# A transformer layer in fp32 on one core: transposes moved between projections, stores queued later, one probability slot given for two activation slots

## What is computed

```
xn  = (x - mean) / sqrt(var + 1e-5)                        per token
q, k, v = split(xn @ w_qkv + b_qkv);  16 heads of 16
a   = softmax(q k^T / 4, keys j >= i only) @ v
s   = a @ w_out + b_out
h   = 2 relu(s0 * [xn, -xn] @ (+-1 from k0))               512 -> 1024
h   = 2 relu(s1 * h @ (+-1 from k1))                       1024 -> 1024
g   = silu(s2 * h @ (+-1 from k2))                         1024 -> 256
out = x + s * g
```

## Time and profile before

| | |
|---|---|
| median of three runs | 2287.67 us (2287.02 to 2289.31) |
| the profiled execution | 2290.6 us, of which its span 2288.8 us |
| PE busy | 2219.8 us, 97% of the span |
| DVE, ACT, POOL busy | 78%, 69%, 40% |
| chain that ended last, by engine | PE 85%, DMA 4%, DVE 4%, issue 2%, POOL 2%, ACT 1%, SP queue 1% |
| first chain item of the projections | DMA a_xs<-L_attn_x, 3% of the span |
| moved | 193.31 MB, mean 84 GB/s |

### The profile page before, as it was taken

The page is one execution under the profiler, slowest core; times in us unless marked ns, Lnnn a source line. Parts: engine busy times, 40 slices in busy tenths (PEclk is TensorE's granted clock), DMA queues, the critical chain, the costliest instruction groups (busy, mean ns, idle before and its releaser), DMA issues.

```text
span 2288.8 us, 60916 instructions
## 1 busy us (share of the span) xinstructions
PE 2219.8 (97%) x23760; PEld 1579.6 (69%) x23760; DVE 1783.3 (78%) x4484; ACT 1569.0 (69%) x3199; POOL 908.2 (40%) x1080
## 2 busy tenths in 40 slices
PE   7998999999999999999999999999999999999987
PEld 6787776667676766666666666777666767776653
DVE  7774788888888878788878878787878788887742
ACT  5663467777777776667777767777777677777554
POOL 1004434333442454335344443444354443445534
PEclk9999999999999999999999999999999999999988
DMA  8995111111121312222222213122222222123132
GB/s 299 350 330 178 32 33 43 43 53 44 42 54 30 99 38 78 56 55 68 58 81 62 77 46 98 39 81 51 67 72 57 67 62 82 48 83 89 53 94 83
DMA packets 157844, 193.31 MB, mean 84 GB/s; under 512 B 65276, under 2 KB 102076, under 8 KB 157560
## 3 DMA queue, kind: packets, MB, share of 16 engines
q1 hardware_dynamic: 156600, 189.41, 27.1%
q10 hardware_dynamic: 960, 0.00, 0.0%
HBM read 112.13 MB, written 76.14 MB: 82 GB/s over the span
## 4 chain that ended last, share of the span: by engine, by line
PE 85%; DMA 4%; DVE 4%; issue 2%; POOL 2%; ACT 1%; SPq 1%; ACTq 0%; POOLq 0%; DVEq 0%
PE b_ps L1423 26%; PE b_pv_ps L1389 22%; PE b_ps L1360 15%; PE b_ps L1370 12%; PE b_ps L1419 5%; DMA a_xs<-L_attn_x 3%; PE b_ps L1444 2%; PE a_qk_ps L291 1%; DVE b_part_max L1535 1%; DVE a_stats L397 1%; DVE a_qk_parts L435 1%; PE b_ps L1377 1%; ACT b_u L1509 1%; ACT b_probs L1478 1%; POOL b_u_lo L1292 0%
## 5 line engine op out<-in xcount | busy, mean ns | idle before, releaser
L1478 ACT ACTIVATE b_probs<-b_ps 128x512 f32<-128x512 f32 (+3 forms) x2560 | 1248.9, 540 | 566.4 <-PE b_ps L1360 532.5
L1535 DVE TENSOR_REDUCE b_part_max<-b_ps 128x1 f32<-128x512 f32 x1536 | 967.8, 682 | 187.4 <-PE b_ps L1370 181.8
L1360 PE MATMUL b_ps<-k_qst,k_kst 50*128 50x512 f32 (+3 forms) x2560 | 907.6, 389 | 8.7 <-DMA k_qst<-b_max_parts 7.2
L1370 PE MATMUL b_ps<-k_kst,k_qst 48*128 48x512 f32 (+3 forms) x2560 | 900.6, 391 | 8.7 <-DMA k_qst<-qk_parts 2.9
L1360 PEld LDWEIGHTS b_ps<-k_qst,k_kst 50*128 50x128 f32 x2560 | 445.4, 186 | 254.5 <-issue 93.0
L1532 DVE CUSTOM_DVE_ANT_0 b_ps<-b_ps,k_mask 128x512 f32<-128x512 f32 (+3 forms) x1024 | 481.5, 515 | 159.3 <-PE b_ps L1370 149.4
L1423 PE MATMUL b_ps<-b_u_hi,k_w 64*128 64x256 f32 x4096 | 594.1, 282 | 1.1 <-ACT b_u L1509 0.7
L1423 PE MATMUL b_ps<-b_u_lo,k_w 64*128 64x256 f32 x4096 | 587.3, 280 | 0.0
L1389 PE MATMUL b_pv_ps<-b_probs,k_vst 128*32 128x512 f32 (+3 forms) x5120 | 567.6, 539 | 3.6 <-issue 2.7
L1370 PEld LDWEIGHTS b_ps<-k_kst,k_qst 48*128 48x128 f32 x2560 | 438.6, 185 | 105.4 <-issue 28.1
L1423 PEld LDWEIGHTS b_ps<-b_u_hi,k_w 64*128 64x128 f32 x4096 | 464.5, 187 | 23.1 <-issue 6.4
(11 more groups left out here) (102 smaller groups left out, 1906.5 us busy)
## 6 DMA issues: line engine op xcount, KB each, us to landing
qk_parts<-a_qk_parts SPq DMA_DIRECT2D x64, 512.0 KB, 3.8
k_kst<-qk_parts SPq DMA_DIRECT2D x384, 64.0 KB, 2.3
k_qst<-qk_parts SPq DMA_DIRECT2D x384, 64.0 KB, 2.3
a_xs<-L_attn_x SPq DMA_DIRECT2D x16, 512.0 KB, 6.1
xn_T<-a_xT SPq DMA_DIRECT2D x16, 512.0 KB, 5.9
v_plain<-a_v_out SPq DMA_DIRECT2D x16, 512.0 KB, 5.7
k_xf<-xn_T SPq DMA_DIRECT2D x32, 256.0 KB, 3.3
b_v_in<-v_plain SPq DMA_DIRECT2D x64, 128.0 KB, 2.7
```

The source lines that it names most:

```text
L1360: pe.matmul(dst[:, 0:cols], keys, qst[rows, c, pair, 0:cols], start=True, stop=True).then_inc(s_ready, 1)
L1370: pe.matmul(dst[:, 0:CHUNK - k1], qst[rows, c, pair, i * P:(i + 1) * P], kst[rows, k_slot(kc, g % 2), pair, k1:CHUNK], start=True, stop=Tr ...
L1478: act.activation(probs[:, s % P_SLOTS, h, 0:cols], ps[:, banks[place, 0][0], 0:cols], ACT.Exp, scale=HD ** -0.5).then_inc(exp_done, 1)
L1535: dve.tensor_reduce(dst, src, AX_X, ALU.max).then_inc(ring_read, 1)
```

## The change

In the first stage the transposes of chunk i+1 and the high copies that go with them move in between the q/k groups (before m = 2; in chunk 0 before m = 3), and DVE's `split_x(i + 1)` moves from behind `deviation` to in front of `low(2)`. A token tile is turned when it is normalised, not when all four are. The first x is loaded in four transfers with a semaphore each; the split of chunk 0 and the whole copy of it come before the statistics and the deviation of chunk 1. In the second stage SP's stores of the gate and of the result leave the place of the work that makes them: they come 3 and 4 steps later, or just before the next "fetch", "fetch_last" or "gate" if that is sooner. `P_SLOTS` goes from 5 to 4, `U_SLOTS` from 2 to 4.

```diff
--- before.py
+++ after.py
@@ -170,6 +170,7 @@
         w_ready = sem("w_ready")
         blank = sem("blank")
         x_loaded = [sem(f"x_loaded{n}") for n in range(2)]
+        x_first = [sem(f"x_first{t}") for t in range(TT)]
         waited = sem("waited")
         ln_stat, ln_aggr, ln_step = sem("ln_stat"), sem("ln_aggr"), sem("ln_step")
         var_ready, std_ready = sem("var_ready"), sem("std_ready")
@@ -187,6 +188,10 @@
 
         x_t = x.rearrange("b s h -> (b s) h")
 
+        def turn_at(i):
+
+            return KH if i > 0 else 2 * KH - 1
+
         def over_chunks(chunk):
 
             for i in range(NCHUNK):
@@ -198,7 +203,8 @@
                 src = x_t[j * CHUNK:(j + 1) * CHUNK, :].rearrange("(t p) h -> p t h", p=P)
                 sp.dma_start(xs[par][:], src).then_inc(x_loaded[par], DMA)
 
-            load_x(0, 0)
+            for t in range(TT):
+                sp.dma_start(xs[0][:, t, :], x_t[t * P:(t + 1) * P, :]).then_inc(x_first[t], DMA)
             sp.dma_start(wqkv[:], w_qkv.rearrange("(k p) f -> p k f", p=P)).then_inc(wqkv_loaded, DMA)
             load_x(1, 1)
             sp.dma_start(k0s[:], k0.rearrange("(a k p) f -> p (a k) f", a=2, p=P)
@@ -269,15 +275,16 @@
         @block.tensor
         def _(pe):
             def turn(j, par):
-                pe.wait_ge(xn_ready, (j + 1) * TT)
                 if j > 0:
 
                     pe.wait_ge(xT_copied, j * KH)
-                for ft in range(KH):
-                    for t in range(TT):
+                for t in range(TT):
+                    pe.wait_ge(xn_ready, j * TT + t + 1)
+                    for ft in range(KH):
                         mm = pe.transpose(turned[:, ft, t * P:(t + 1) * P], xs[par][:, t, ft * P:(ft + 1) * P],
                                           kept.identity[:])
-                    mm.then_inc(turned_ready, 1)
+                        if t == TT - 1:
+                            mm.then_inc(turned_ready, 1)
 
             products = [(k, w, part) for k in range(KH)
                         for w, part in ((wqkv_hi, xT_hi), (wqkv_hi, xT_lo), (wqkv_lo, xT_hi))]
@@ -285,14 +292,14 @@
             def chunk(i, half, par, left):
                 pe.wait_ge(xT_low, (i + 1) * KH)
                 for m in range(2 * KH):
+                    if m == turn_at(i) and left:
+                        turn(i + 1, 1 - par)
 
                     pe.wait_ge(qk_low, i * 2 * KH + m + 1)
                     for n, (k, w, part) in enumerate(products):
                         mm = pe.matmul(qk_ps[:, m], w[:, k, m * P:(m + 1) * P], part[par][:, k, :],
                                        start=(n == 0), stop=(n == len(products) - 1))
                     mm.then_inc(qk_ready, 1)
-                if left:
-                    turn(i + 1, 1 - par)
                 for u in range(VU):
                     pe.wait_ge(v_done, i * VU + u + 1)
                     for t in range(2):
@@ -321,6 +328,8 @@
                 act.sem_inc(qk_stored[par], QK_STORES * DMA)
                 act.sem_inc(v_stored[par], DMA)
                 act.sem_inc(xT_stored[par], DMA)
+
+            act.sem_inc(x_loaded[0], DMA)
 
             def std_of(j):
                 act.wait_ge(var_ready, j + 1)
@@ -356,13 +365,13 @@
             def chunk(i, half, par, left):
                 act.wait_ge(qk_stored[par], (half + 1) * QK_STORES * DMA)
                 for m in range(2 * KH):
+                    if m == turn_at(i) and left:
+                        copy_high(i + 1, 1 - par)
                     act.wait_ge(qk_ready, i * 2 * KH + m + 1)
                     act.activation(qk_parts[par][:, m, HI, :], qk_ps[:, m], ACT.Identity,
                                    bias=bqk[:, m:m + 1]).then_inc(qk_high, 1)
                 if left > 1:
                     std_of(i + 2)
-                if left:
-                    copy_high(i + 1, 1 - par)
                 act.wait_ge(v_stored[par], (half + 1) * DMA)
                 for u in range(VU):
                     act.wait_ge(v_ready, i * VU + u + 1)
@@ -377,8 +386,8 @@
             act.wait_ge(wqkv_loaded, DMA)
             act.activation(wqkv_hi[:], wqkv[:], ACT.Copy).then_inc(wqkv_split, 1)
             copy_high(0, 0)
+            copy_whole(0, 0, 0)
             std_of(1)
-            copy_whole(0, 0, 0)
             act.wait_ge(consts, 3)
             act.wait_ge(biases_loaded, DMA)
             over_chunks(chunk)
@@ -394,6 +403,8 @@
                 if tokens[0] == 0:
                     dve.wait_ge(x_loaded[par], (half + 1) * DMA)
                 for t in tokens:
+                    if j == 0:
+                        dve.wait_ge(x_first[t], DMA)
                     dve.bn_stats(stats[:, t, :], xs[par][:, t, :]).then_inc(ln_stat, 1)
 
             def variance(j):
@@ -443,15 +454,14 @@
                 low(1)
                 if ahead:
                     statistics(i + 2, half + 1, par, (2, 3))
+                if left:
+                    split_x(i + 1, 1 - par)
                 low(2)
                 if ahead:
                     variance(i + 2)
                 low(3)
                 if ahead:
                     deviation(i + 2)
-                if left:
-                    split_x(i + 1, 1 - par)
-                if ahead:
                     scaled(i + 2, par, range(TT))
                 if KH <= i < 2 * KH:
 
@@ -463,13 +473,12 @@
             for j in range(2):
                 statistics(j, 0, j, range(TT))
                 variance(j)
-                if j == 1:
-                    split_x(0, 0)
                 deviation(j)
                 scaled(j, j, range(TT))
                 if j == 0:
                     dve.wait_ge(wqkv_split, 1)
                     dve.tensor_tensor(wqkv_lo[:], wqkv[:], wqkv_hi[:].bitcast(F32), ALU.subtract).then_inc(wqkv_split, 1)
+                    split_x(0, 0)
             dve.wait_ge(biases_loaded, DMA)
 
             dve.wait_ge(scales_loaded, 3 * DMA)
@@ -494,8 +503,8 @@
 
 
 KB = S // P
-P_SLOTS = 5
-U_SLOTS = 2
+P_SLOTS = 4
+U_SLOTS = 4
 SIG_PARTS = 8
 
 PV_LAG, M_LEAD = 2, 21
@@ -733,8 +742,25 @@
                     self.clock["POOL"] += {"finish": 2.5, "finish_last": 2.5, "scale": 1.3, "place_v": 0.5, "gate": 1.3}[what]
                 elif what in ("recip", "invert"):
                     self.clock["DVE"] += 0.48
+                if what in ("fetch", "fetch_last", "gate"):
+                    self.leave()
                 self.end_span()
                 self.emit(what, *args)
+                self.store_later(what, *args)
+
+    def store_later(self, what, *args):
+
+        if what == "gate":
+            self.later(self.step() + 3, 0.0, "store_gate", *args)
+        elif what == "finish" and args[2] == 1:
+            self.later(self.step() + 4, 0.0, "store_y", *args[:2])
+
+    def leave(self):
+
+        self.end_span()
+        for event in [e for e in self.side if e[2] in ("store_gate", "store_y")]:
+            self.side.remove(event)
+            self.emit(*event[2:])
 
     def whole_array(self):
 
@@ -852,7 +878,10 @@
                 self.end_span()
                 for event in [e for e in self.side if e[2] in ("recip", "gate")]:
                     self.side.remove(event)
+                    if event[2] == "gate":
+                        self.leave()
                     self.emit(*event[2:])
+                    self.store_later(*event[2:])
             for n in range(F_BANKS):
                 self.take(("F", self.use, n), "f")
         taken = [self.banks["F", self.use, n][0] for n in range(F_BANKS)]
@@ -1037,7 +1066,7 @@
         sum_of, wo_last = xf[:, 0, 0:P], xf[:, 1, 0:H]
         last_inv = z[:].rearrange("p t h -> p (t h)")
 
-        last_xs = u[:].rearrange("p s t n -> p (s t) n")
+        last_xs = u[:, 0:2].rearrange("p s t n -> p (s t) n")
         last_gates = (sig[:], gt[:])
 
         bv_wide = heads_T[:, :, 0:P]
@@ -1208,11 +1237,10 @@
                     sp.dma_start(tokens(out_t, LAST_CHUNK)[:, rows], last_xs[:, rows]).then_inc(y_stored, DMA)
                 elif what == "project":
                     uses += 1
-                elif what == "finish":
-                    e, i, half = arg
-                    if half == 1:
-                        sp.wait_ge(y_ready, 2 * (e + 1))
-                        sp.dma_start(tokens(out_t, i), xs[:]).then_inc(y_stored, DMA)
+                elif what == "store_y":
+                    e, i = arg
+                    sp.wait_ge(y_ready, 2 * (e + 1))
+                    sp.dma_start(tokens(out_t, i), xs[:]).then_inc(y_stored, DMA)
                 elif what == "load_x":
                     k, = arg
                     r = pieces[k]
@@ -1221,7 +1249,7 @@
                         sp.wait_ge(x_split, k)
                     src = scratch.xT[r // PPC, :, :, r % PPC * PIECE:(r % PPC + 1) * PIECE]
                     sp.dma_start(xf[:], src).then_inc(x_loaded, DMA)
-                elif what == "gate":
+                elif what == "store_gate":
```

## The result

The changed kernel takes 2286.43 us (median of 12 runs, 2283.63 to 2289.92), the kernel before 2289.32 us in the same session: a ratio of 0.9983, with an interval of 0.9975 to 0.9992. That is 2 to 6 us faster, and inside the 0.2% that I had set as "same". I had forecast 2293.8 us, slower. The profiled execution has a span of 2286.4 us against 2288.8.

The account below looks back on a forecast made before the run. It took the x-load ring to bound the projections and TensorE the attention. Terms +5.7 + 0.1 - 0.4 + 0.7 = +6.1 us on the 2287.67 us median gave 2293.8 us, slower; 8-in-10 range 2281 to 2302.

Parts of the forecast that it names:

- The ring: Projections: x load, DVE work, stores, next load; split of x adds 1.20 us, turns become 10.75 us, +5.7 us over 13.
- the empty queue: Projections: rival that the x load finds an empty queue, 4.4 us, turn 9.85 us, total 2282 us; chance 0.20.
- no relief: Projections: rival that the x load keeps its 6.0 us and all 1.20 us count, +14.8 us, 2303 us; chance 0.17.
- the row at 27.08 us: Profile row of the first x load in the projections' cycle, behind little-delayed stores, landing in 5.5 us; basis for 5.3.
- the alone one: Profile row of an x load with no store near it, landing in 3.8 us; basis for the 4.4 us lower end.
- One sign: Projections: TensorE's waits should be at the transposes, for normalised x, and not at the low part.
- The start: Before the first repeating x load: four-part x, but DVE busy and w_qkv later; +0.1 us, bounds -1.5 and +1.
- The hand-over: Behind chunk 13, projections to attention: TensorE gains 2 to 3 us, stores limit it; 0.4 us gain, bounds 0 to 2.
- The slots: Attention: four places for P and u cost and gain 0; Plan's possibly changed order 0, with 3 us to both sides.
- The stores in the middle of the attention: SP's 318.1 us before the gate's store delays nobody in mid-attention; moving the stores matters at the end only, 0.
- The end: Last rows of maxima leave SP 1.5 us later, gate store gives TensorE 0.8; sum +0.7 us, bounds -6 and +2.
- the end opens: Rival: Plan puts the last rows of maxima before "fetch_heads", TensorE gets back 6.3 us, 2287 us; chance 0.13.

## Why the prediction was wrong

**The ring** was right in place, mechanism and size: landing to issue 5.45 us, loads 5.1 (5.3 forecast), turns 10.72 (10.75), the place +4.95 us (+5.8 with the start). The rivals of the empty queue and of no relief are out: the load settled between the row at 27.08 us and the alone one. One sign was missed: TensorE still waited 6.5 us in 12 waits for the low part of x, and at the transposes 3.2 us for ACT's whole copy and not for the normalised x. The share of the transfer engines was 0.91 to 0.96 in windows of 20 us (0.93 or 0.94 forecast). The Trainium skill's formula (DMA: Bandwidth & Descriptors, "Anatomy of one DMA — SWDGE (gpsimd) path") would give 3.2 us as an estimate; the section gives it for transfers that GpSimd issues, and these are SP's, which the prediction did not say. The traces do not agree with it: no load of the ring landed in under 5.0 us in the changed kernel, or under 4.6 in any kernel. One baseline was soft, though. The first stage of before ends at 161.09 us in its profile, and at 158.08, 158.19 and 159.83 us in three kernels with the same code of it. The loss of the stage is 5 to 8 us, and the start, -0.5 us here, is +0.3 to +1.1 against those three.

**The start**: -0.5 us instead of +0.1. **The hand-over** to the attention: +0.2 instead of -0.4. **The slots**: 0 forecast, nothing in the middle, perhaps 1 to 3 us behind 2080 us. The fifth place was never used, as read from Plan's order.

**The stores in the middle of the attention** are the step that failed: "TensorE shows no wait worth a us for what SP sends", priced at 0. I had read a window in which TensorE is full and taken it for all. The stage had two windows of 50 us, from 850 and from 1000 us, with TensorE busy 48.1 and 48.0 of them, and the list of waits had one of 1.9 us for a load of q. I also valued the 318.1 us that SP stood before the gate's store by asking who waits for that store, and not what stands behind it in the queue: loads of q and k, and copies of heads that ACT waits for. Measured, the two middle stalls are 4.0 us (5.13 to 1.14), and 4.0 and 4.1 with the stores or the gate's store alone. Without them the forecast would have been 2 us slower than before instead of 6, still not faster. The rest of the miss is 3.5 us at the end and the 0.7 us of the one execution of before.

**The end**: +0.7 us forecast with -6 as its bound. The piece that I worked out is there: the last rows of maxima wait 8.56 us against 7.20, 1.4 us more (1.5 forecast), because their store now comes behind two loads. But three things were missing: 2.8 us won from 2082 to 2149 us, where q of the last group is no longer behind the store of the result; 2.7 us up to 2211 us, where I had only 0.8 from the gate's store (that store alone gives 0.7 there, both stores 2.1); and 2.7 us lost behind it, the 1.4 and a wait for POOL that grew from 4.85 to 6.45 us:

```profile
2220.41 1.65 PE L1388 MATMUL b_ps<-k_qst,k_kst 50*128 50x512 f32 x5 [8.56 <-DMA k_qst<-b_max_parts]
...
2263.17 3.75 PE L1472 MATMUL b_ps<-b_wo,b_heads_T 128*128 128x256 f32 x8 [6.45 <-POOL b_heads_T L1355]
```

The order at the end stayed as it was, so the rival "the end opens" did not come by itself; and where an experiment opened it, it gave nothing and not 6.3. I had priced a wait at its own length, not at the distance to the next one.

Together: +5.13 (stage, start, hand-over) - 3.99 - 0.72 - 2.82 - 2.67 + 2.67 = -2.40 us, the difference of the spans. The 0.72 us is the stall that only this execution of the kernel before has; the change did not win it. Not settled: why the same first stage differs by 3 us from one profile to the next, how large the gains behind 2082 us are from one execution to another, and how much of the few us at the end is the order that Plan writes with the new slots. The parts measured alone (+3, -9 and -3 us by the ratios) also do not add up to the -4 of the whole, though their intervals, of 2 to 3 us to each side, nearly cover it.

## What to carry to other kernels

Before pricing an edit in an in-order transfer queue, list for each long wait what stands behind it and who waits for that; a full engine in one window says nothing of the three or four places in two milliseconds where it is not. Where a load's own order keeps it in a ring, look for the earliest moment at which its buffer is free and issue it there: moving work in or out of the ring was worth 5 us, taking the load out of it 20. And follow one instruction that stands once in every round through both traces: a constant difference that jumps names the stalls at once. Do it with a third and a fourth kernel too: a jump that all of them show is a stall of the one execution they are compared with.

## What was unexpected of the hardware

The transfer engines kept up with 9.31 us a chunk, at 382 to 406 GB/s and shares of 1.00 to 1.03 in five windows of 20 us, where at 10.3 us a chunk they had already shown 0.97 and 361 GB/s: a share near 1 did not tell how much faster they could go. And a load's time went with what was queued near it, 3.8 us alone, 5.1 with a gap before it, 6.0 in the full ring and 6.5 in the kernel where it no longer mattered.
